# A graph layer with residual and layer norm: x transposed a unit ahead, dense products first, bias added on VectorE

## The reference

```
row, col = src, dst                                # 50,000 edges, sorted by dst
msg = concat([x[row], edge_attr], 1) @ W1 + b1     # 64 + 32 -> 128
agg = segment_sum(msg, col, 100000)                # 100,000 nodes
y   = x + (concat([x, agg], 1) @ W2 + b2)          # 64 + 128 -> 64
out = (y - mean(y)) / sqrt(var(y) + 1e-5)          # over the 64 columns
```

## Time and profile before

| | us |
|---|---|
| median of 3 runs | 690.79 (686.96 to 691.35) |
| the profiled execution | 688.16 |
| its span | 686.4 |
| TensorE matmul busy | 548.4 (80%) |
| TensorE weight load busy | 503.7 (73%) |
| VectorE busy | 428.0 (62%) |
| GpSimd busy | 425.7 (62%) |
| ScalarE busy | 394.1 (57%) |

### The profile page before, as it was taken

The page is one execution under the profiler, slowest core; times in us unless marked ns, Lnnn a source line. Parts: engine busy times, 40 slices in busy tenths (PEclk is TensorE's granted clock), DMA queues, the critical chain, the costliest instruction groups (busy, mean ns, idle before and its releaser), DMA issues. The chain is left out here.

```text
span 686.4 us, 26310 instructions
## 1 busy us (share of the span) xinstructions
PE 548.4 (80%) x8174; PEld 503.7 (73%) x8175; DVE 428.0 (62%) x961; ACT 394.1 (57%) x2012; POOL 425.7 (62%) x421
## 2 busy tenths in 40 slices
PE   1457879989889988988888988988886978876573
PEld 1345868888888888888888888887875867765552
DVE  2679447777777767767767777675764554454433
ACT  0001365777777777777777777777775545342211
POOL 6777727677677777777677777777777755000000
PEclk9999597999999999999999999999998777786855
DMA  2123324564555465564554664564634433131102
GB/s 65 33 33 34 72 71 104 138 155 112 149 148 141 118 162 125 130 160 109 143 144 110 153 161 120 132 154 102 162 95 97 108 72 88 38 93 34 32 2 62
DMA packets 171917, 71.38 MB, mean 104 GB/s; under 512 B 64737, under 2 KB 165615, under 8 KB 171888
## 3 DMA queue, kind: packets, MB, share of 16 engines
q1 hardware_dynamic: 107728, 51.75, 26.2%
q0 software_dynamic: 12544, 12.87, 10.5%
q10 hardware_dynamic: 51616, 6.41, 6.0%
HBM read 45.37 MB, written 25.60 MB: 103 GB/s over the span
## 5 line engine op out<-in xcount | busy, mean ns | idle before, releaser
L416 POOL DMA_INDIRECT feat<-in_x,src_idx x392 | 416.7, 1063 | 151.6 <-issue 122.8
L638 ACT ACTIVATE square<-ps_y 128x64 bf16<-128x64 f32 x784 | 162.1, 238 | 95.9 <-PE ps_y L517 90.1
L526 PEld LDWEIGHTS ps_y<-z_window,onehot 128*128 128x128 bf16 x5484 | 181.0, 100 | 27.6 <-DVE z_window L877 13.4
L526 PE MATMUL ps_y<-z_window,onehot 128*128 128x64 bf16 x5484 | 185.5, 196 | 9.1 <-DVE z_window L877 9.0
L882 DVE TENSOR_TENSOR onehot<-node_of_col,dst_in_group 128x2304 bf16<-128x2304 bf16 x98 | 134.4, 1372 | 69.5 <-issue 61.4
L638 ACT ACTIVATION_READ_ACCUMULATOR square<-ps_y 128x1 f32 x784 | 159.1, 224 | 0.0
L517 PE MATMUL ps_y<-wx,x_t 128*128 128x128 f32 x784 | 117.0, 294 | 43.1 <-ACT x_t L630 36.9
L517 PEld LDWEIGHTS ps_y<-wx,x_t 128*128 128x128 f32 x784 | 99.1, 198 | 48.9 <-ACT x_t L630 41.7
L602 ACT ACTIVATE feat_t<-ps_t 97x512 f32<-97x512 f32 x98 | 58.6, 598 | 106.8 <-PE ps_z L449 79.4
L449 PE MATMUL ps_z<-wz,feat_t 97*128 97x64 f32 x784 | 108.8, 299 | 11.7 <-DVE z_rest L757 11.7
L449 PEld LDWEIGHTS ps_z<-wz,feat_t 97*128 97x128 f32 x784 | 106.1, 217 | 14.3 <-DVE z_rest L757 9.7
(11 more groups left out here) (137 smaller groups left out, 242.5 us busy)
## 6 DMA issues: line engine op xcount, KB each, us to landing
xin<-in_x SPq DMA_DIRECT2D x97, 192.0 KB
out<-yout SPq DMA_DIRECT2D x97, 192.0 KB
xin<-in_x SPq DMA_DIRECT2D x99, 64.0 KB
out<-yout SPq DMA_DIRECT2D x99, 64.0 KB
feat<-in_x,src_idx POOLq DMA_INDIRECT x392
feat<-in_edge_attr ACTq DMA_DIRECT2D x97, 64.0 KB
z<-in_src SPq DMA_DIRECT2D x1, 192.0 KB
z<-in_dst SPq DMA_DIRECT2D x1, 192.0 KB
```

The lines of the kernel that those rows point to most:

```text
L416: nc.gpsimd.indirect_dma_start(out=feat[h][:, feat_at(k) + c, 0:C], out_offset=None, in_=x[:, :], in_offset=bass.IndirectOffsetOnAxis(ap=s ...
L526: mm = nc.tensor.matmul(ps_y[h][:, col:col + C], onehot[h][:, slot, a, :], z_window[h][:, slot, part * C:(part + 1) * C], start=False, sto ...
L638: sq = nc.scalar.activation(square[:, q, :], ps_y[h][:, q * C:(q + 1) * C], ACT.Square, accum_out=sumsq[:, h, q:q + 1])
```

## The change

In each unit TensorE does the dense product of a half first, from an `x_t` that is already there, then transposes the x of the next unit into `ps_x[h]`, then does the one-hot matmuls; the last of these ends the half. The bias matmul and its tables `b2rows` and `ones_bf` are gone: b2 is loaded by one broadcast DMA into `b2_row`, and VectorE adds it as it copies y from PSUM to `y_sb` (`keep_y`, now on VectorE). ScalarE no longer copies y; it squares `y_sb`. The halves are staggered: in unit u VectorE first adds b2 to half 1 of the unit before, and last to half 0 of this one; ScalarE squares half 1 of the unit before, takes the root for that unit, copies the next unit's x, and squares half 0 of this one. `normalize(u)` still handles unit u-1, but now waits for `root(u)`. SP's loop has the same order of calls; the transposes that free `xin` come a unit earlier. The start values of some semaphores change with this (`x_ready`, `y_kept`, `squared`), and the first x is transposed and copied ahead of the loop. The counts of the set-up's semaphores fall from 8 to 7, 16 to 14 and 8 to 6.

The diff, cut to what the prediction speaks of (declarations, and the set-up of b2 on 65 rows that becomes one on 128, are left out):

```diff
@@ -300,8 +297,7 @@
                 sp.dma_start(wx[r * C:(r + 1) * C, r * C:(r + 1) * C], W2[0:C, :]).then_inc(s_wload, 16)
-            for r in range(3):
-                sp.dma_start(b2c[32 * r:32 * r + 1, :], b2.rearrange("(o f) -> o f", o=1)).then_inc(s_wload, 16)
+            sp.dma_start(b2_row[:, :], b2.rearrange("(o f) -> o f", o=1).to_broadcast([P, C])).then_inc(s_wload, 16)
             def load_x(k, h):
...
@@ -343,9 +339,13 @@
             for k in range(1, PAIRS + 1):
-                if k < PAIRS:
-                    for h in range(2):
+                for h in range(2):
+                    if k < PAIRS:
                         load_x(k, h)
+                    else:
+                        sp.wait_ge(x_used[h], PAIRS)
+                        sp.sem_inc(x_loaded[h], 32)
                 if k >= 2:
...
@@ -363,8 +363,7 @@
             nc.gpsimd.memset(wx[:, :], 0.0).then_inc(s_clear, 1)
-            nc.gpsimd.memset(b2c[:, :], 0.0).then_inc(s_clear, 1)
-            nc.gpsimd.memset(std[:, :, :], 1.0).then_inc(s_clear, 1)
+            nc.gpsimd.memset(sumsq[:, :, :], 0.0).then_inc(s_clear, 1)
             nc.gpsimd.memset(xin[0][:, :, :], 0.0).then_inc(s_clear, 1)
...
@@ -429,7 +426,6 @@
                 pe.sem_inc(hotx_used[s])
-                pe.sem_inc(hots_used[s])
                 pe.sem_inc(y_done[s])
...
@@ -464,8 +460,8 @@
-            pe.wait_ge(s_wload, 16 * 8)
-            pe.wait_ge(s_const, 16)
+            pe.wait_ge(s_wload, 16 * 6)
+            pe.wait_ge(s_const, 14)
             nc.tensor.transpose(ps_a[0:H, 0:F], w1aug[:, :], ident[0:F, 0:F]).then_inc(s_w, 1)
...
@@ -499,7 +495,7 @@
                 pe.wait_ge(x_loaded[h], 16 * transfers(k + 1, h))
-                pe.wait_ge(x_ready[h], k + 1)
+                wait_rounds(pe, x_ready[h], k)
                 for g in range(G):
...
@@ -509,26 +505,25 @@
                 pe.wait_ge(y_kept[h], k + 1)
-                pe.wait_ge(squared[h], k + 1)
-                nc.tensor.matmul(ps_y[h][:, :], ones_bf[:, :], b2rows[:, :, :].rearrange("p n c -> p (n c)"),
-                                 start=True, stop=False)
-                def dense(g):
-                    return nc.tensor.matmul(ps_y[h][:, g * A * C:(g + 1) * A * C], x_t[h][:, g * P:(g + 1) * P],
-                                            wx[:, :], start=False, stop=(g == G - 1))
-                def slots_sum(g, chunks):
+                pe.wait_ge(x_ready[h], k + 1)
+                for g in range(G):
+                    nc.tensor.matmul(ps_y[h][:, g * A * C:(g + 1) * A * C], x_t[h][:, g * P:(g + 1) * P],
+                                     wx[:, :], start=(g == 0), stop=False)
+                turn_x(k + 1, h)
+                def slots_sum(g, chunks, last=False):
                     for slot in range(SLOT[g], SLOT[g] + chunks):
                         for a in range(A):
                             col = (g * A + a) * C
                             for part in range(3):
                                 mm = nc.tensor.matmul(ps_y[h][:, col:col + C], onehot[h][:, slot, a, :],
-                                                      z_window[h][:, slot, part * C:(part + 1) * C], start=False, stop=False)
+                                                      z_window[h][:, slot, part * C:(part + 1) * C], start=False,
+                                                      stop=(last and slot == SLOTS - 1 and a == A - 1 and part == 2))
                     return mm
                 pe.wait_ge(hot_ready, b + 1)
-                for g in range(G):
+                for g in range(G - 1):
                     pe.wait_ge(window_ready, G * b + g + 1)
...
@@ -559,15 +554,10 @@
                                         mm.then_inc(hotx_used[s], 1)
-                pe.wait_ge(x_ready[h], k + 2)
-                dense(0).then_inc(hots_used[h], 1)
-                for g in range(1, G - 1):
-                    dense(g)
-                dense(G - 1).then_inc(y_done[h], 1)
+                pe.wait_ge(window_ready, G * b + G)
+                slots_sum(G - 1, TAKEN[G - 1], last=True).then_inc(y_done[h], 1)
             def unit(u):
-                for h in range(2):
-                    turn_x(u, h)
                 for h in range(2):
...
@@ -583,6 +573,8 @@
             pe.wait_ge(s_wready, 3)
+            for h in range(2):
+                turn_x(0, h)
             pe.wait_ge(s_loaded_steps, 32)
...
@@ -626,46 +618,38 @@
                 act.wait_ge(x_used[h], u + 1)
-                act.wait_ge(y_done[h], u + 1)
                 nc.scalar.activation(x_t[h][:, :], ps_x[h][:, :], ACT.Copy).then_inc(x_ready[h], 1)
-            def keep_y(u, h):
-                act.wait_ge(y_done[h], u + 2)
-                act.wait_ge(squared[h], u + 1)
-                act.wait_ge(squared[1 - h], u + 1 + h)
-                act.wait_ge(s_root, u + 1)
+            def square_sums(u, h):
+                act.wait_ge(y_kept[h], u + (2 if h == 0 else 1))
+                act.wait_ge(squared[1 - h], u + 1)
+                act.wait_ge(s_root, u + (2 if h == 0 else 1))
                 for q in range(G * A):
-                    sq = nc.scalar.activation(square[:, q, :], ps_y[h][:, q * C:(q + 1) * C], ACT.Square,
-                                              accum_out=sumsq[:, h, q:q + 1])
+                    sq = nc.scalar.activation(square[:, q, :], y_sb[h][:, q, :], ACT.Square, accum_out=sumsq[:, h, q:q + 1])
                 sq.then_inc(squared[h], 1)
-                act.wait_ge(out_ready[h], u + 1)
-                nc.scalar.activation(y_sb[h][:, :, :], ps_y[h][:, :].rearrange("p (n c) -> p n c", c=C),
-                                     ACT.Copy).then_inc(y_kept[h], 1)
             def root(u):
+                act.wait_ge(squared[0], u + 1)
+                act.wait_ge(squared[1], u + 1)
+                act.wait_ge(s_rstd, u + 1)
+                nc.scalar.activation(std[:, :, :], sumsq[:, :, :], ACT.Sqrt, bias=eps[:, :], scale=1.0 / C).then_inc(s_root, 1)
+            def unit(u):
+                square_sums(u, 1)
+                root(u)
                 for h in range(2):
-                    act.wait_ge(squared[h], u + 2)
-                act.wait_ge(s_rstd, u + 2)
-                nc.scalar.activation(std[:, :, :], sumsq[:, :, :], ACT.Sqrt, bias=eps[:, :], scale=1.0 / C).then_inc(s_root, 1)
-            def unit(u):
-                for h in range(2):
-                    keep_x(u, h)
-                for h in range(2):
-                    keep_y(u, h)
-                root(u)
+                    keep_x(u + 1, h)
+                square_sums(u, 0)
             act.sem_inc(s_root)
-            for h in range(2):
-                act.sem_inc(x_ready[h])
-                act.sem_inc(y_kept[h])
-                act.sem_inc(squared[h])
-            act.wait_ge(s_clear, 8)
+            act.sem_inc(squared[0])
+            act.wait_ge(s_clear, 7)
             for h in range(2):
                 load_ea(0, h)
-            act.wait_ge(s_const, 16)
+            act.wait_ge(s_const, 14)
             nc.scalar.activation(std_eps[:, :], eps[:, :], ACT.Sqrt)
...
@@ -683,6 +667,8 @@
             z_mids(LAG - 1)
+            for h in range(2):
+                keep_x(0, h)
             act.wait_ge(s_loaded_steps, 32)
...
@@ -699,6 +685,8 @@
                 for_units(act, mybir.EngineType.Activation, k - LAG, unit)
+            square_sums(PAIRS, 1)
+            root(PAIRS)
...
@@ -713,6 +701,7 @@
             dve.sem_inc(s_rstd)
+            dve.sem_inc(y_kept[0])
             dve.wait_ge(s_iload, 16 * 7)
...
@@ -831,15 +820,6 @@
             dve.wait_ge(s_wready, 2)
-            for n in range(3):
-                link(nc.vector.tensor_copy(b2part[:, n, :], b2c[:, :]))
-                if n < 2:
-                    link(nc.vector.tensor_tensor(b2r[:, :], b2c[:, :], b2part[:, n, :], ALU.subtract))
-                    link(nc.vector.tensor_copy(b2c[:, :], b2r[:, :]))
-            for n in range(3):
-                for q in range(G * A):
-                    nc.vector.tensor_copy(b2rows[32 * n:32 * n + 1, q, :], b2part[32 * n:32 * n + 1, n, :])
             bases = group_base[:, :].rearrange("p (b g o) -> p b g o", g=G, o=1)
...
@@ -872,7 +852,7 @@
                           for g, f in enumerate(firsts)]
-                dve.wait_ge(hots_used[h], k + 1)
+                dve.wait_ge(y_done[h], k + 1)
                 def window_of(g, at, chunks, ready):
...
@@ -910,22 +890,35 @@
+            def keep_y(u, h):
+                dve.wait_ge(y_done[h], u + (2 if h == 0 else 1))
+                nc.vector.tensor_tensor(y_sb[h][:, :, :], ps_y[h][:, :].rearrange("p (n c) -> p n c", c=C),
+                                        b2_row[:, :].rearrange("p (o c) -> p o c", o=1).to_broadcast([P, G * A, C]),
+                                        ALU.add).then_inc(y_kept[h], 1)
             def normalize(u):
-                dve.wait_ge(s_root, u + 1)
+                dve.wait_ge(s_root, u + 2)
```

(19 more changed lines are left out.)

10 lines of the change are left out of this document (3 added, 7 removed).

## The result

The changed kernel takes **828.41 us** (median of 4 runs, 824.22 to 832.54); the kernel before took 690.02 (median of 4): a ratio of 1.201, 95% interval 1.193 to 1.210. I had forecast 758. The range that I had stated was 708 to 790. The profiled execution took 824.22 us and spans 822.4.

The account below looks back on a forecast made before the run. Gathers were taken to fill the rounds near 385 us already, and a new ring of waits to set them afterwards: 688.2 + 52 (ring) + 10 (clock) + 9 (behind) - 1.3 (start) = 758 us, range 708 to 790.

Parts of the forecast that it names:

- the ring: Closed chain of waits through z_rest, messages, feature copies, squares, root and outputs: six legs, 11.9 us per round, +52 us.
- step 5: Ring leg on VectorE: new addition 0.70 us, then issue time ahead of z's low part 0.58, up to 0.65 longer.
- step 3: Ring leg on ScalarE: eight squares 1.74 us, then root 0.40; squares from SBUF priced at no extra time.
- the clock's term: TensorE idle near 3 us per round lowers its clock: 1.6 us in each of six rounds, +10 us.
- the dense products' place: Dense products first in a half, with x ahead: claimed to remove TensorE's x wait, 0.97 us each; no cost named.
- Behind the rounds: Units after 509 us without edge work: VectorE's two additions each cost 6 to 13 us, taken as +9.
- x loads on SP: Loads of x now come behind the stores of the unit before; a round to land, priced at 0.
- The start: Set-up without the 24 bias-row copies and nine instructions ahead of them: 1 to 2.5 us won, taken as -1.3.
- Bias matmul: 98 matmuls of 0.40 us removed from TensorE: worth nothing with gathers at 11 us per round, no cover lost.
- The gathers: GpSimd's queue, eight gathers per round, is never free and alone would hold the 35 rounds near 385 us.
- "faster" rival: Root not late, TensorE's x wait gone, gathers shorten toward their median: about 10.4 us per round, 666 us; chance 0.08.

Follow-up runs that it names:

- e2: Changed kernel with VectorE's wait for its own second output moved from the unit's end to ahead of its first use a unit later; 774.4 us.
- e4: Changed kernel with the feature transposes of the loop's rounds done three times, so TensorE idles less; 803.8 us.
- e13b: Changed kernel with dense products and x transposes last in each half, ScalarE's half 0 squares ahead of the next x copies; 802.1 us.
- e11: Changed kernel with squares and root early on ScalarE, second-output wait a unit later, dense products and x transposes last, half 0 squares before x copies; 693.6 us.
- e5b: Kernel before with x a unit ahead and dense products first; bias matmul, ScalarE's y copy and the root's old place stay; 721.0 us.
- e10: Kernel before with x a unit ahead, dense products left last, next x's transposes behind them, ScalarE's x copies after the root; 680.9 us.
- e7: Kernel before with six of each round's eight gathers; 686.8 us.
- e12b: Kernel before with x a unit ahead, dense products last, and six of each round's eight gathers; 645.8 us.
- e3: Changed kernel with half 1's squares and the root of a round's first unit moved ahead of ScalarE's edge copies; 756.5 us.
- e8b: Changed kernel with the edits of e2 and e3 together, dense products still first; 713.8 us.

## Why the prediction was wrong in size

The direction (0.84 for slower) and the ring were right, and four of its six legs came out within 0.01 us. The forecast was 70 us too low and the time lies above the whole range. The steps that failed are step 5 and step 3 of the ring, the clock's term, and the dense products' place, which had no term. By the prediction's own steps:

**Step 5 of the ring, the issue time.** I took 0.58 plus 0.3, at most 1.23. It is 1.75. I had seen that VectorE now waits for its second output before it goes on, but priced only half an overlap; e2 shows that 1.03 us of the gap come from that wait. With the output and addition 0.09 shorter than their rows, the leg is 0.78 longer, 27 us in 35 rounds. This is the largest failed term.

**Step 3, the squares.** I took the same length from SBUF as from PSUM. The rows' lengths would say so still, 0.24 against 0.22 to 0.27, but from start to start it is (358.75 - 357.06) / 7 = 0.241 us now and was (310.93 - 309.54) / 7 = 0.199 before. With the root it is 0.30 per round, 10.5 us in 35. The Trainium skill ("VectorE: DVE Perf Modes", section on the TRN2 errata) had charged 0.04 us more per square and 12 us in all; the trace agrees (0.042), and it should have been in the sum.

**The clock.** Ten us, six slow rounds, was too few: ten of the first 31 rounds were 13.8 or longer, and e4 gives back 24.6 us, 11 in the rounds and 10 behind, where I had none. The price of one, 1.6, was right (14.46 less 12.96 is 1.5). The picture was not: I expected one idle piece of some 3 us per round ahead of the messages. The fast round has 0.94 us there, 0.58 ahead of the feature transposes and 0.15 between the halves, since issue gaps behind the slots split the idle time; before the messages it was 1.25 on average (35.1 in 28 waits), 2.6 at most. Even so the clock fell in most rounds, and what it cost depended on whether the low stretch lay on the messages. With the dense products last (e13b) the idle time is mostly in one piece, 2.4 us on average (65.5 in 27 waits, 150 to 550 us).

**Behind the rounds.** Nine us from the additions; measured 25.3. The additions explain little of it: in e11, which has them, 3.5 us are left. The dense products' place, with ScalarE's order that goes with it, accounts for 20.8 (e13b), and I had priced it at nothing.

**Dense products first, the step that has no term.** I named only what it removes, TensorE's wait for x. The cover that the dense products gave to TensorE's issue time at the end of a half is gone; e5b stands 31 us above the kernel before with x ahead's gain already in it, and 40 above e10. Inside the ring it hides (2.6 us in the rounds of e13b).

**x loads on SP, priced at nothing.** TensorE waited 10.7 us in five waits for x in the whole run: 1.1 at the start, 3.5 in the two double rounds, 6.1 behind the rounds, nothing in a round with one unit. Nothing per round was right; the 9.6 of the other two places belonged to the upper end of the range. The start was 4.1 us later instead of 1.3 earlier: the set-up was shorter (the first z_rest at 66.76 instead of 67.85), but the first units lost more.

**Bias matmul, worth nothing.** Not tried alone. No run here shows what it is worth; in e10, where TensorE has hardly any idle time in a single round, it may count.

**The gathers.** "The gathers alone would hold this stretch near 385 us even if TensorE waited for nothing": e10 took that wait away and measured 384.7. Right, though e7 shows that the wait for x held it just as well. My "faster" rival, 666, would have needed both: the wait for x gone and fewer or shorter gathers (e12b: 645.8).

The terms together: the rounds were forecast 62 us longer and are 106.6 longer. Of the 45 missing, 27 are step 5, 10.5 step 3 and some 6 the clock. With 16 behind and 5 at the start that is 66, the distance of 758 from the profiled execution (688.2 and the 136.0 of the spans). The other 4 us up to 828.4 are the median's distance from that execution.

## What to carry to other kernels

Price the gap behind an engine's wait for its own output as the whole issue time of what follows, and where such waits and a root close a ring over all engines, look for the one order on one engine that makes a link late (here e3's). Long matmuls at a block's end can hide the issue time of the next block; before they are moved, ask what else will, and price the two halves of a double change apart (x ahead was worth 1.4%; dense first cost 6% between e10 and e5b, 3% between e11 and e8b and between e13b and the changed kernel). When a wait fits a kernel's pace, a second limit of the same length may stand beside it, and only removing both shows it.

## What was not expected of the hardware

- A sequence of 54 short bf16 matmuls (1.74 us) left 0.9 us of issue time open behind it; the same with eight float32 products (1.14 us) and four transposes (0.60) behind it left none. That TensorE's reading of its tables is what takes the time is argued, not shown.
- Small activations with a sum: from SBUF 0.241 us from start to start, from PSUM 0.199, while the recorded lengths of both are near 0.24.
- Of five chips, three ran the kernel before in 689 to 691 us and two in 1057 and 1069, where TensorE's slot matmuls came with 0.4 to 1.2 us of issue between them; six gathers instead of eight made kernels there 12 to 13% faster. The cause is open.
- One low stretch of TensorE's clock costs 1.5 us when it lies on the messages (3.56 us instead of 2.00) and nothing when it lies on the products and slots of the same round (2.48 us instead of 1.74).
